# Relative-position bias carried as extra contraction rows of the query and key stacks, with a tanh gate

## The chip, the cores and the metric

One core of one Trainium2 chip runs the kernel. The metric is the device time of the whole launch in microseconds, all 16 batch entries included. Engines are named as the profile names them: PE (TensorE), PEld (its weight loads), DVE (VectorE), ACT (ScalarE), POOL (GpSimd), SP (SyncE, which issues the DMAs).

## The reference

The input x is 16 batches of 16 particles by 48 times by 128 channels. Each batch is one sequence of 768 tokens.

1. LayerNorm over the channels, then attention with 8 heads of 16 dimensions. The score of a query and a key is q·k/4 plus a bias that depends on their time distance plus a bias that depends on their particle distance, each with its own value per head. Keys at a later time than the query are masked. Softmax, product with v, output projection, residual.
2. LayerNorm, then a feed-forward part with 8 experts: softmax over 8 gate logits, the two largest kept and normalised to sum 1. For each of the two weights w, every expert computes GELU(w·x·W1 + b1)·W2, and all are summed. Residual.

## The kernel before

All tokens of a batch lie in time order, so a tile of 128 tokens is 8 times by 16 particles, and there are six tiles. The feed-forward part of one batch is 64 "units" (2 token chunks by 8 experts by 4 slices of the hidden dimension). The attention of the next batch is cut into steps, and a written-out list, `PLAN` (L44 to L66), gives each step the slot (unit number) at which every engine does its share. So the steady state is a loop of 64 slots per batch in which unit work and attention steps alternate in a fixed order on each engine. The first batch's attention runs alone before that loop (it is called the solo batch below), and the last batch's feed-forward part runs alone behind it.

A unit is three matmuls into `zps` (L893 to L895), a multiply on DVE (L727), two GELUs on ACT (L532, L533), an add on POOL (L445) and six matmuls into `acc` (L904).

The attention steps that matter here:

- **stack** (L357): for each of four heads of a group, five DMAs on SP's queue put the head's query and key rows, each as a high and a low fp32r half, in four combinations into `stack` (64 contraction rows, and two rows for the maxima).
- **maxima** (L803 PE, L648 DVE): matmuls give the query-by-key tile without bias. DVE adds the bias and mask from a table `query_table` and takes the row maximum in one custom instruction (L656). Three parts per head, in two PSUM buffers `wide0` and `wide1` that all wide steps use by turns.
- **rows** (L814 PE, L492 ACT, L660 DVE, L377 SP): the maxima of four heads are transposed, negated, split into high and low, and sent by two DMAs into two rows of the query stack.
- **scores** (L817 PE, L496 ACT): key-by-query tiles, three parts per head. Every tile takes two matmuls, one of the stack (L827) and one that adds the bias (L830, one-hot keys times `bias_rows`). ACT takes the exponential (L504). Group 0 stands wholly in slot 26, group 1 in slot 44: no unit work lies between its twelve parts.
- **mix**, **sums**, **divide**, **project**: product with v, denominators, division, output projection.
- **gate**, **weigh**, **split** (L678 to L714): DVE sorts the eight logits and subtracts the largest, ACT takes the exponential (L516), eight small DVE instructions form the two weights, DVE scales xn, PE transposes it (L878, L879) and ACT and DVE split it for the next batch's units.

Ahead of the loop, `query_table` is made by PE and DVE (L764, L576), the bias rows by DVE, POOL and ACT (L560 to L563, L436, L540, L288), and both weights of the experts are loaded.

Of the kernel before, what the change touches and what calls it, by code (L numbers as in the profile page):

```python
# [5 lines left out]
F32 = mybir.dt.float32  # L6
# [3 lines left out]
ALU = mybir.AluOpType  # L10
# [20 lines left out]
STACK_DMAS = 5  # L31
QCOLS = 512
ZW = 2688
NEG = -1e30
LN_EPS = (1e-6, 1e-5)
# [43 lines left out]
VCHAIN = 2 * (5 + 3 * NEWTON) + 7  # L79
# [23 lines left out]
def build(nc, x, Wq, Wk, Wv, Wo, time_bias, part_bias, Wg, W1, b1, W2, b2, out):  # L103
    with ExitStack() as ctx:
# [6 lines left out]
        def sem(name):  # L111
# [15 lines left out]
        bias_rows = sb("bias_rows", [P, GH, TOK], F32R)  # L127
        key_hot = sb("key_hot", [P, GROUPS, P], F32R)
        query_table = sb("query_table", [P, HEADS, TOK], BF16)

# [9 lines left out]
        stack = sb("stack", [P, 2, GH, TOK], F32R)  # L140
        qst, kst = stack[:, 0], stack[:, 1]
# [3 lines left out]
        max_rows = sb("max_rows", [GH * TILES, 2, P])  # L145
# [6 lines left out]
        sorted_l, shifted, gate_e = (halves[:, 3, QCOLS + 48 * n:QCOLS + 48 * (n + 1)].rearrange(  # L152
            "p (i e) -> p i e", e=EXPERTS) for n in range(3))
        gate_s = sb("gate_s", [P, TILES, 4])
        probs = sb("probs", [P, TILES, 2])
# [18 lines left out]
        w1_stage = z[:, 0, 0:2048], z[:, 1, 0:2048]  # L174
        one_hot = z[0:48, 2, 0:128]
        hot_stage = z[0:48, 2, 128:256]

        z_flat = z[:, :, :].rearrange("p g c -> p (g c)")
        raw = [w2[:, 0:GH * TOK // C, :].rearrange("p e d -> p (e d)").rearrange("p (h t) -> p h t", h=GH), z_flat[:, 6912:6912 + GH * TOK].rearrange("p (h t) -> p h t", h=GH)]
        t_stage = z[0:8, 2, 256:256 + 48 * 8]  # L180
        p_stage = z[32:48, 2, 256:256 + 16 * 8]
        b2_stage = z[0:8, 2, 768:896]
        twos = z[0:8, 2, 896:1024]
        b1_stage = z[0:32, 2, 1024:1152]
        rel_stage = z_flat[0:48, 9984:9984 + TOK]
        rel = [rel_stage[:, n * TOK // 2:(n + 1) * TOK // 2].bitcast(BF16) for n in range(2)]

        bias_hi = [w[:, :, :].rearrange("p e f -> p (e f)")[:, 0:GH * TOK].rearrange("p (h t) -> p h t", h=GH)
                   for w in (w1_hi, w1_lo)]
        one_hot16 = z[0:48, 2, 1152:1152 + P // 2].bitcast(BF16)  # L190

        biases_loaded = sem("biases_loaded")
        weights_loaded = sem("weights_loaded")
        w1_high = sem("w1_high")
# [4 lines left out]
        raw_ready = sem("raw_ready")  # L199
        raw_masked = sem("raw_masked")  # L200
        rel_ready = sem("rel_ready")
        bias_high = sem("bias_high")
        bias_low = [sem("bias_low0"), sem("bias_low1")]
        bias_placed = sem("bias_placed")
        table_filled = sem("table_filled")
        table_used = sem("table_used")
        setup_filled = sem("setup_filled")
        setup_done = sem("setup_done")
# [11 lines left out]
        rows_high = sem("rows_high")  # L220
        rows_loaded = sem("rows_loaded")
# [59 lines left out]
        def lower_biases(eng, g):  # L281

            for n, (row, count) in enumerate(((0, TPT), (32, PARTS))):
                eng.wait_ge(bias_high, 2 * g + n + 1)
                if n:
                    eng.wait_ge(bias_low[g], n)
                rows = slice(row, row + count)
                eng.tensor_tensor(raw[g][rows, :, :], raw[g][rows, :, :], bias_hi[g][rows], ALU.subtract).then_inc(bias_low[g], 1)  # L288

# [12 lines left out]
        def _(sp):  # L302
# [13 lines left out]
            for dst, src in ((wqkv[:, 0, :], Wq), (wqkv[:, 1, :], Wk), (wqkv[:, 2, :], Wv), (wg[:, :], Wg)):  # L316
                sp.dma_start(dst, src).then_inc(weights_loaded, 16)
                n += 1
# [81 lines left out]
        def _(pool):  # L400
# [49 lines left out]
            def prepare(r, step, a):  # L450
# [6 lines left out]
                elif (step, a) == ("turn", 1):  # L457
                    for a in range(2):
                        pool.wait_ge(w1_high, a + 1)
                        if a:  # L460
                            pool.wait_ge(w1_low, a)
# [472 lines left out]
```

## Time and profile before

| what | value |
|---|---|
| median of 3 runs | 2730.64 us (2728.61 to 2734.73) |
| the profiled execution's own time | 2739.47 us |
| its span | 2737.6 us |
| mean granted TensorE clock | 0.957 |
| busy share PE, PEld, DVE, ACT, POOL | 87%, 78%, 54%, 62%, 40% |
| the chain that ended last, by engine | PE 57%, DVE 17%, issue 13%, ACT 9%, DMA 2% |

The span runs from the first to the last instruction. A busy share is a mean over stages with different limits, and a pipelined matmul counts as busy from its issue to its modelled end, so that matmuls overlap. "idle before, releaser" in a row is the time that the engine stood still ahead of that instruction, and whose end let it go on. The granted clock is 1.00 at 2.4 GHz and 0.50 at 1.2 GHz.

### The profile page before, as it was taken

The page shows a single profiled execution, that of the slowest core. Times are in us where ns is not written, and L with a number is a line of the kernel's source. Part 1 is how long each engine was busy: PE and PEld are TensorE (multiplying, and loading weights), DVE is VectorE, ACT ScalarE, POOL GpSimd, SP SyncE. Part 2 cuts the span into 40 slices and gives each one's busy share as a digit, 9 for nine tenths or more (in the row PEclk, how much of TensorE's full clock was granted, in tenths as well). Part 3 has the DMA queues.
Part 4 walks back from the last instruction along what each step waited for, and adds up shares of the span by engine and source line. Part 5 has one row for each costly group of instructions (what it writes and reads, how often), then busy time and mean ns, then how long its engine had stood idle before and what let it go on. Part 6 is the DMA issues. An engine that isn't in the chain of part 4 may idle for free.

```text
span 2737.6 us, 57322 instructions
## 1 busy us (share of the span) xinstructions
PE 2377.7 (87%) x18611; PEld 2127.1 (78%) x18611; DVE 1469.6 (54%) x4157; ACT 1695.3 (62%) x2788; POOL 1089.9 (40%) x1054
## 2 busy tenths in 40 slices
PE   1567989899898989989899898989989898998989
PEld 0347878788887878888787878878887787888878
DVE  7536365444735545474554636544573554547454
ACT  2125656675675666666566665667566566756667
POOL 6004244343433434343343424434352443434347
PEclk9678999999999999999999999999999999999999
DMA  2411212040221303022030212203022120302200
GB/s 34 73 38 25 28 28 34 7 52 7 31 28 20 42 7 43 13 34 28 10 49 10 31 25 34 28 8 51 10 28 28 24 38 7 44 12 34 28 10 7
DMA packets 62802, 74.34 MB, mean 27 GB/s; under 512 B 16192, under 2 KB 43744, under 8 KB 62432
## 3 DMA queue, kind: packets, MB, share of 16 engines
q1 hardware_dynamic: 62528, 70.68, 18.4%
q8 instruction: 173, 2.83, 0.4%
q14 instruction: 101, 0.83, 0.1%
HBM read 11.19 MB, written 6.29 MB: 6 GB/s over the span
## 4 chain that ended last, share of the span: by engine, by line
PE 57%; DVE 17%; issue 13%; ACT 9%; DMA 2%; POOL 1%; SPq 1%; DVEq 0%; POOLq 0%; ACTq 0%
PE acc L904 15%; PE wide L827 6%; PE narrow L844 6%; PE zps L893 6%; ACT z L504 5%; PE wide L830 5%; DVE wide L656 5%; PE zps L895 4%; PE zps L894 4%; PE wide L811 4%; DVE h L727 2%; PE wide L865 2%; PE wide L851 1%; DMA stack<-stack 1%; DVE maxes L656 1%
## 5 line engine op out<-in xcount | busy, mean ns | idle before, releaser
L445 POOL TENSOR_TENSOR hsum<-h 128x384 f32<-128x384 f32 x1024 | 1030.2, 1010 | 1491.9 <-ACT h L533 1477.3
L727 DVE TENSOR_TENSOR h<-zps,ratio_b 128x384 f32<-128x384 f32 x1024 | 561.8, 555 | 921.1 <-PE zps L895 917.3
L532 ACT ACTIVATE h<-zps,b_col 128x384 f32<-128x384 f32 x1024 | 594.3, 580 | 662.4 <-DVE h L727 637.1
L904 PE MATMUL acc<-w,hsum 128*128 128x128 f32 x6144 | 867.3, 278 | 1.4 <-DVE outt L736 1.2
L904 PEld LDWEIGHTS acc<-w,hsum 128*128 128x128 f32 x6144 | 850.2, 195 | 2.2 <-POOL hsum L445 1.7
L533 ACT ACTIVATE h<-h,b_col 128x384 f32<-128x384 f32 x1024 | 620.7, 606 | 0.0
L893 PE MATMUL zps<-x_hi,w_lo 128*128 128x384 f32 x1024 | 426.5, 416 | 100.7 <-ACT h L532 57.6
L656 DVE CUSTOM_DVE_ANT_0 wide<-wide,query_table 128x768 f32<-128x768 f32 (+5 forms) x768 | 461.6, 649 | 46.7 <-PE wide L811 44.0
L827 PE MATMUL wide<-stack 128*128 128x256 f32 (+3 forms) x1280 | 374.7, 323 | 69.9 <-ACT z L504 33.9
L504 ACT ACTIVATE z<-wide 128x896 f32<-128x896 f32 (+2 forms) x384 | 345.3, 918 | 95.1 <-PE wide L830 94.3
L894 PE MATMUL zps<-x_lo,w_hi 128*128 128x384 f32 x1024 | 353.4, 345 | 0.0
L895 PE MATMUL zps<-x_hi,w_hi 128*128 128x384 f32 x1024 | 352.6, 344 | 0.0
L830 PE MATMUL wide<-bias_rows,key_hot 128*128 128x256 f32 (+3 forms) x1280 | 351.4, 307 | 0.0
L827 PEld LDWEIGHTS wide<-stack 128*128 128x128 f32 x1280 | 253.1, 198 | 120.0 <-ACT z L504 74.6
L893 PEld LDWEIGHTS zps<-x_hi,w_lo 128*128 128x128 f32 x1024 | 199.2, 195 | 144.1 <-ACT h L532 79.2
L811 PE MATMUL wide<-stack 128*128 128x512 f32 (+3 forms) x1024 | 259.3, 362 | 17.4 <-DVE maxes L656 8.8
L830 PEld LDWEIGHTS wide<-bias_rows,key_hot 128*128 128x128 f32 x1280 | 254.1, 199 | 6.8
L811 PEld LDWEIGHTS wide<-stack 128*128 128x128 f32 x1024 | 168.3, 196 | 43.2 <-DVE maxes L656 20.1
L894 PEld LDWEIGHTS zps<-x_lo,w_hi 128*128 128x128 f32 x1024 | 200.1, 195 | 0.4
L895 PEld LDWEIGHTS zps<-x_hi,w_hi 128*128 128x128 f32 x1024 | 198.1, 193 | 0.0
L844 PE MATMUL narrow<-z,val 128*32 128x256 f32 (+3 forms) x2560 | 175.9, 393 | 3.5 <-ACT mixed L513 1.4
L844 PEld LDWEIGHTS narrow<-z,val 128*32 128x32 f32 x2560 | 82.9, 109 | 87.5 <-issue 21.8
(110 smaller groups left out, 1609.2 us busy)
## 6 DMA issues: line engine op xcount, KB each, us to landing
stack<-halves SPq DMA_DIRECT2D x512, 96.0 KB
x_in<-in_x SPq DMA_DIRECT2D x136, 48.0 KB, 2.4
out_dram<-outt SPq DMA_DIRECT2D x256, 24.0 KB, 1.6
stack<-stack SPq DMA_DIRECT2D x128, 6.0 KB
z<-in_L_ffn_W SPq DMA_DIRECT2D x8, 256.0 KB, 4.2
stack<-max_rows SPq DMA_DIRECT2D x64, 12.0 KB
bias_rows<-w_hi SPq DMA_DIRECT2D x1, 192.0 KB
bias_rows<-w SPq DMA_DIRECT2D x1, 192.0 KB
```

The source lines that it names most:

```text
L445: pool.tensor_tensor(hsum[:, m % NHS, :], h0[:, m % 2, :], h1[:, m % NH1, :], ALU.add).then_inc(hsum_ready, 1)
L532: act.activation(h0[:, m % 2, :], zps[m % 2][:, 0:CT], ACT.Gelu, bias=b1_col[:, j:j + 1]).then_inc(h0_ready, 1)
L533: act.activation(h1[:, m % NH1, :], h1[:, m % NH1, :], ACT.Gelu, bias=b1_col[:, j:j + 1]).then_inc(h1_ready, 1)
L656: ins = vec.tensor_tensor_reduce(w[:, at:at + n], w[:, at:at + n], query_table[:, h, TOK - n:TOK], 1.0, -3e38, ALU.add, ALU.max, maxes[:, ...
L727: vec.tensor_tensor(h1[:, m % NH1, :], zps[m % 2][:, 0:CT], ratio_b[:, c * CT:(c + 1) * CT], ALU.mult).then_inc(z1_ready, 1)
L811: ins = pe.matmul(w[:, at:at + k1 - k0], qst[:, hh, i * P:(i + 1) * P], kst[:, hh, k0:k1], start=True, stop=True)
L827: pe.matmul(w[:, at:at + q1 - q0], kst[:, hh, i * P:(i + 1) * P], qst[:, hh, q0:q1], start=True, stop=False)
L830: ins = pe.matmul(w[:, at:at + q1 - q0], key_hot[:, g, :], bias_rows[:, hh, q0 - i * P:q1 - i * P], start=False, stop=True)
L893: pe.matmul(zp, lo, x0_hi[:, cols], start=True, stop=False)
L894: pe.matmul(zp, hi, x0_lo[:, cols], start=False, stop=False)
L895: pe.matmul(zp, hi, x0_hi[:, cols], start=False, stop=True).then_inc(z_filled, 1)
L904: ins = pe.matmul(acc[:, n * P:(n + 1) * P], hsum[:, k % NHS, n * P:(n + 1) * P], w2[:, j, :], start=(j == 0 and n == 0), stop=(j == UNITS ...
```

## The change

- The query stack becomes eight heads wide (one buffer per head) and holds 127 or 128 contraction rows: 48 rows of data (three high/low combinations in place of four), then bias rows, then one row for the maxima. Time bias: three sets of 16 rows (8 high, 8 low), one for each place of a tile within a half of the tokens. Particle bias: 15 high and 15 low rows. The key stack holds the matching one-hot rows, the same for all batches. A later time has -1e30 in its time row, so the mask is in the product as well.
- The one-hot keys repeat after half of the tokens, so the query stack has a second copy of its second half behind the first, with other time rows; tiles 3 to 5 of the keys meet that copy.
- scores: one matmul per tile. maxima: nine matmuls per head (before eight) with the same number of columns, and a plain maximum on DVE with no table. The six parts of a head are paired so that each part has 896 columns.
- rows: ACT alone, one row, but two DMAs for each head (eight per group). stack: six DMAs for each head. The scores of a head wait only for that head's rows.
- gate: ACT takes tanh of half the difference of the two largest logits; four small DVE instructions in place of eight.
- setup: small tables, spread by ACT and DVE, and placed by 12 DMAs after the solo batch's `value` step; W1 is loaded behind the solo batch's stacks into `w2`, converted on ACT before the solo batch's rows; W2 is loaded after that.

```diff
@@ stack, on SP
-                    for n, (q, k) in enumerate(((0, 2), (1, 2), (0, 3), (1, 3))):
-                        sp.dma_start(stack[n * HD:(n + 1) * HD, :, hh, :].bitcast(F32),
-                                     window(halves[rows, q, :], 0, [[(k - q) * TOK, 2], [1, TOK]])).then_inc(stack_loaded[hh], 16)
-                    sp.dma_start(qst[4 * HD:4 * HD + 2, hh, :].bitcast(F32),
-                                 qst[4 * HD + 2:4 * HD + 4, hh, :].bitcast(F32)).then_inc(stack_loaded[hh], 16)
+                    for n, (q, k) in enumerate(((0, 2), (1, 2), (0, 3))):
+                        to = slice(n * HD, (n + 1) * HD)
+                        sp.dma_start(window(stack[to, :].bitcast(F32), to_q, [[to_k - to_q, 2], [1, TOK]]),
+                                     window(halves[rows, q, :], 0, [[(k - q) * TOK, 2], [1, TOK]])).then_inc(stack_loaded[hh], 16)
+                    for n, q in enumerate((0, 1, 0)):
+                        sp.dma_start(qst[n * HD:(n + 1) * HD, h, TOK:QW].bitcast(F32),
+                                     halves[rows, q, HALF:TOK]).then_inc(stack_loaded[hh], 16)
@@ rows, on SP
-                    for s in range(2):
-                        sp.dma_start(qst[64 + s:65 + s, :, :].bitcast(F32).rearrange("p g (i t) -> p (g i) t", t=P),
-                                     max_rows[:, s, :]).then_inc(rows_loaded, 16)
+                    for hh in range(GH):
+                        row = qst[MAX_ROW:MAX_ROW + 1, a * GH + hh, :].bitcast(F32).rearrange("p (i t) -> p i t", t=P)
+                        sp.dma_start(row[:, 0:TILES, :], max_rows[hh * TILES:(hh + 1) * TILES, :]).then_inc(rows_loaded[hh], 16)
+                        sp.dma_start(row[:, TILES:TILES + HT, :],
+                                     max_rows[hh * TILES + HT:(hh + 1) * TILES, :]).then_inc(rows_loaded[hh], 16)
@@ maxima, on DVE
-                    for i, at in (((5, 0), (1, 768)), ((4, 0), (2, 640)), ((3, 0), (0, 512)))[part]:
-                        n = (i + 1) * P
-                        ins = vec.tensor_tensor_reduce(w[:, at:at + n], w[:, at:at + n],
-                                                       query_table[:, h, TOK - n:TOK], 1.0, -3e38, ALU.add, ALU.max,
-                                                       maxes[:, hh * TILES + i:hh * TILES + i + 1])
+                    for i, at in (((0, 0), (5, P)), ((4, P), (1, 6 * P)), ((3, P), (2, 5 * P)))[part]:
+                        ins = vec.tensor_reduce(maxes[:, hh * TILES + i:hh * TILES + i + 1], w[:, at:at + (i + 1) * P], AX.X, ALU.max)
@@ scores, on PE
-                        pe.matmul(w[:, at:at + q1 - q0], kst[:, hh, i * P:(i + 1) * P], qst[:, hh, q0:q1],
-                                  start=True, stop=False)
-                        ins = pe.matmul(w[:, at:at + q1 - q0], key_hot[:, g, :], bias_rows[:, hh, q0 - i * P:q1 - i * P],
-                                        start=False, stop=True)
+                        shift = HALF if i >= HT else 0
+                        ins = pe.matmul(w[:, at:at + q1 - q0], kst[:, hh, i * P:(i + 1) * P],
+                                        qst[:, g * GH + hh, q0 + shift:q1 + shift], start=True, stop=True)
@@ gate, on ACT
-                    act.activation(gate_e[:, :, :], shifted[:, :, :], ACT.Exp).then_inc(gate_exped, 1)
+                    act.activation(gate_t[:, :], gate_d[:, :], ACT.Tanh, scale=0.5).then_inc(gate_exped, 1)
@@ setup: SP behind the solo batch's value step, DVE behind its LayerNorm
+                if (step, a) == ("value", 0):
+                    sp.wait_ge(times_spread, 1)
+                    ...
+                            sp.dma_start(qst[rows, :, 0:TOK].bitcast(F32), src[:, :, at:at + TOK]).then_inc(bias_placed, 16)
+                            sp.dma_start(qst[rows, :, TOK:QW].bitcast(F32), src[:, :, at:at + HALF]).then_inc(bias_placed, 16)
+                    for h in range(HEADS):
+                        c = h % GH
+                        sp.dma_start(wo_pad[32 * c:32 * c + HD, h // GH, :], Wo[h * HD:(h + 1) * HD, :]).then_inc(wo_loaded, 16)
+                elif (step, a) == ("stack", (0, GH - 1)):
+                    for e in range(EXPERTS):
+                        sp.dma_start(w1_stage[:, e, :], W1[e]).then_inc(w1_loaded, 16)
+                if (step, a) == ("scale", (0, 1)):
+                    vec.tensor_copy(spread[0:40, :, PAD:PAD + TOK].rearrange("p h (t n) -> p h t n", n=PARTS),
+                                    window(t_hl, (TIMES - 1) * HEADS, [[1, HEADS], [-HEADS, TIMES], [0, PARTS]])
+                                    ).then_inc(times_spread, 1)
```

## Rows read from the trace of the kernel before

**Rows 1.** The page's part 5, groups: busy us, mean ns, idle before, releaser

```profile
L656 DVE CUSTOM_DVE_ANT_0 wide<-wide,query_table 128x768 f32<-128x768 f32 (+5 forms) x768 | 461.6, 649 | 46.7 <-PE wide L811 44.0
...
L504 ACT ACTIVATE z<-wide 128x896 f32<-128x896 f32 (+2 forms) x384 | 345.3, 918 | 95.1 <-PE wide L830 94.3
...
L830 PE MATMUL wide<-bias_rows,key_hot 128*128 128x256 f32 (+3 forms) x1280 | 351.4, 307 | 0.0
```

**Rows 2.** The chain that ended last: project step, second and last, 14 apart

```profile
351.82 2.68 PE wide L865 x24
...
2620.81 2.68 PE wide L865 x24
```

**Rows 3.** Timeline of ACT in one round's scores of group 1: start, us

```profile
1296.66 1.68 ACT L504 ACTIVATE z<-wide 128x896 f32<-128x896 f32 x2
...
1302.14 1.92 ACT L504 ACTIVATE z<-wide 128x1024 f32<-128x1024 f32 x2 [0.19 <-PE wide L830]
1304.39 0.81 ACT L504 ACTIVATE z<-wide 128x768 f32<-128x768 f32 x1 [0.34 <-PE wide L830]
...
1308.65 1.02 ACT L504 ACTIVATE z<-wide 128x1024 f32<-128x1024 f32 x1 [0.19 <-PE wide L830]
```

**Rows 4.** Timeline of PE in the same round's scores of group 0

```profile
1252.72 0.33 PE L827 MATMUL wide<-stack 128*128 128x256 f32 x1
...
1253.61 0.28 PE L830 MATMUL wide<-bias_rows,key_hot 128*128 128x256 f32 x1
1253.79 0.50 PE L827 MATMUL wide<-stack 128*128 128x512 f32 x1
...
1254.54 0.34 PE L830 MATMUL wide<-bias_rows,key_hot 128*128 128x384 f32 x1
```

**Rows 5.** Windows: length, busy and count by engine, granted clock, DMA share, GB/s

```profile
1246.00:1248.00 2.00, 2.00 (x9) 1.68 (x8) 0.00 (x0) 1.02 (x1) 0.00 (x0) 0.50 0.00 0
...
1302.00:1304.00 2.00, 1.88 (x12) 1.46 (x11) 0.00 (x0) 1.86 (x2) 0.00 (x0) 1.00 0.00 0
...
148.00:152.00 4.00, 2.96 (x9) 2.15 (x8) 3.43 (x12) 0.00 (x0) 0.00 (x0) 0.50 0.00 0
```

**Rows 6.** Timeline of DVE in the same round's maxima of group 1

```profile
1286.17 0.95 DVE L656 CUSTOM_DVE_ANT_0 wide<-wide,query_table 128x768 f32<-128x768 f32 x1
...
1287.04 0.46 DVE L656 CUSTOM_DVE_ANT_0 wide<-wide,query_table 128x256 f32<-128x256 f32 x1
```

**Rows 7.** Timeline around the gate of the same round

```profile
1180.84 1.28 ACT L532 ACT_TABLE_LOAD   x1 [0.32 <-DVE h L727]
...
1182.77 0.45 PE L893 MATMUL zps<-x_hi,w_lo 128*128 128x384 f32 x1 [0.97 <-ACT h L532]
...
1184.07 0.27 PE L878 MATMUL wide<-ident,xn 128*128 128x128 f32 x1
```

**Rows 8.** Timeline of SP's queue and PE at the first stack of a round

```profile
1207.33 2.58 SPq L372 DMA_DIRECT2D stack<-halves  x4
...
1214.26 0.74 PE L811 MATMUL wide<-stack 128*128 128x512 f32 x3 [0.29 <-DMA stack<-stack]
```

**Rows 9.** Timeline of the setup and the solo batch

```profile
7.12 4.22 DVE L560 COPY w<-z 8x3072 f32<-8x3072 f32 x1 [7.12 <-POOL z L423]
...
36.95 1.26 DVE L611 BATCH_NORM_STATS2 act_t<-x_in 128x6 f32<-128x128 f32 x6
...
86.82 2.16 PE L811 MATMUL wide<-stack 128*128 128x512 f32 x6 [5.87 <-issue]
...
106.66 0.27 ACT L494 ACTIVATE max_rows<-wide 24x128 fp32r<-24x128 f32 x1 [42.34 <-PE wide L816]
...
201.08 3.00 DVE L686 TENSOR_TENSOR halves<-halves 128x48 f32<-128x48 f32 x1
...
204.85 3.83 DVE L692 TENSOR_TENSOR probs<-halves,gate_s 128x12 f32<-128x12 f32 x1
```

**Rows 10.** The page's part 6, DMA issues: KB each, us to landing

```profile
z<-in_L_ffn_W SPq DMA_DIRECT2D x8, 256.0 KB, 4.2
```

More of the change, by code:

```diff
@@ L30 @@
 NHS = 4
-STACK_DMAS = 5
 QCOLS = 512
@@ L34 @@
 NEG = -1e30
+STACK_DMAS = 6
+HALF = TOK // 2
+QW = TOK + HALF
+TIME_ROWS = (48, 79, 111)
+PART_ROWS = (64, 96)
+PART_N = PARTS - 1
+MAX_ROW = 127
+PAD = 2 * P
 LN_EPS = (1e-6, 1e-5)
@@ L151, in build @@
         ln_t = sb("ln_t", [P, TILES])
[L152 to L155, printed above, removed]
+        sorted_l = halves[:, 3, QCOLS:QCOLS + 48].rearrange("p (i e) -> p i e", e=EXPERTS)
+        gate_d = sb("gate_d", [P, TILES])
+        gate_t = sb("gate_t", [P, TILES])
+        gate_r = sb("gate_r", [P, TILES])
         top = sb("top", [P, TILES, 2])
@@ L279, in rounds @@
             slots(Round(eng, BATCHES - 1), None, None)
[L281 to L288, printed above, removed]
         def wide_at(r, step, a):
@@ L426, in _ @@
             assert done == POOL_SMALL
+            pool.wait_ge(biases_loaded, 16 * BIAS_LOADS)
+            for row in (0, 32):
+                v = t_tab[row:row + TPT, :].rearrange("p (m h) -> p m h", h=HEADS)
+                pool.affine_select(out=v, in_=v, compare_op=ALU.is_ge, fill=NEG, base=TIMES - 1,
+                                   pattern=[[-1, TIMES], [0, HEADS]], channel_multiplier=-1).then_inc(tables_masked, 1)
             for buf, value in later:
@@ new lines, in _ @@
+            for row in (0, 32):
+                rows = slice(row, row + PART_N)
+                vec.tensor_tensor(p_diff[rows, :], p_tab[rows, :], p_first[rows, :], ALU.subtract).then_inc(parts_less, 1)
+            vec.wait_ge(tables_high, 2)
+            vec.tensor_tensor(t_hl[32:32 + TPT, :].bitcast(F32R), t_tab[32:32 + TPT, :], t_hl[32:32 + TPT, :],
+                              ALU.subtract).then_inc(tables_low, 1)
+            vec.wait_ge(tables_high, 4)
+            vec.tensor_tensor(p_hl[32:32 + PART_N, :].bitcast(F32R), p_diff[32:32 + PART_N, :], p_hl[32:32 + PART_N, :],
+                              ALU.subtract).then_inc(tables_low, 1)
@@ L741, in after @@
                         residual(r, 1)
-            rounds(vec, attention, unit, after, last=("stats", "seed", "root", "scale", "rows"), prepare=prepare)
+            rounds(vec, attention, unit, after, last=("stats", "seed", "root", "scale"), prepare=prepare)
         @block.tensor
@@ L755, in prepare @@
             def prepare(r, step, a):
[L756 to L769 removed]
+                if (step, a) == ("value", 0):
+                    pe.wait_ge(pool_set, POOL_SET)
+                    pe.wait_ge(hots_placed, 16 * HOT_DMAS)
+                    pe.wait_ge(parts_spread, GROUPS)
+                    pe.wait_ge(bias_placed, 16 * BIAS_DMAS)
+                elif (step, a) == ("divide", 1):
+                    pe.wait_ge(wo_loaded, 16 * HEADS)
                 elif (step, a) == PLAN[-1][1:]:
```

269 lines of the change are left out of this document (105 added, 164 removed).

## The prediction

> **What bounds the kernel now.** I read the groups of part 5 first, then the chain that ended last over the whole run and in one steady round, and then the timelines of the stages that the change touches. The groups name three things to follow [rows 1]. ACT's exponential stood idle for 94 us waiting for the bias matmul L830. L830 itself is 351 us of busy PE. The custom maximum on DVE is 462 us. The chain gives the round: 2269.0 us between the first and the last project step of the loop, 14 rounds, so 162.07 us each [rows 2]. Fifteen rounds carry an attention; the solo batch ahead of them and the last feed-forward part behind them make up the rest.
>
> A round is a chain of stages with different limits. In the stages with unit work alone, PE and ACT are both full. In scores nothing lies between the parts: ACT and PE hand two buffers to each other, and the four heads of group 1 take 1308.65 + 1.02 - 1296.66 = 13.01 us, 3.25 per head [rows 3]. In that stage ACT waits 0.34 us ahead of the 768-wide part and 0.19 ahead of the 1024-wide one, so it is the sum of both engines that sets the pace: a buffer is filled, read, and only then filled again. Over two heads each buffer is used three times. Its 6.5 us are three exponentials (the 2.75 us that three times the mean of 918 ns give), three fills, and the hand-overs.
>
> **The change, part by part.**
>
> *Scores, one matmul per tile.* The 1024-wide part has eight matmuls and takes 1253.61 + 0.28 - 1252.72 = 1.17 us, with 0.127 us from one start to the next (0.89 over seven); the 896-wide part has four and takes 1254.54 + 0.34 - 1253.79 = 1.09 us [rows 4]. Half of the matmuls and half of the columns go. In the 1024-wide part that is 4 x 0.127 = 0.51 us; 896 columns at 2.4 GHz are 0.37 us, the lower bound. I take 0.42 per fill. Three fills in two heads: 0.63 us per head, from 3.25 to 2.62. ACT's own floor is near it: 1.68 for two parts back to back plus 1.02 for the third is 2.70, less about 0.05 for each overlap of one with the next (0.92 + 0.81 against 1.68), so 2.6 [rows 3]. Four heads: 2.5 us for each group. Group 1 also waits for its first fill with nothing before it: another 0.4. Group 0 has its first 0.9 us or more of exponential behind a table load, so none there. Together 5.4 us per round; bounds 4.4 (fills cut by 0.37) and 6.3 (by 0.51, ACT nearly never waiting).
>
> This part depends on the clock. In group 0 PE already drops to 0.50 for some microseconds in the middle of scores, after standing idle behind the table load, and comes back with PE busy all the time; in group 1 it stays at 1.00 with 1.88 of 2.00 us busy; and in the solo batch's maxima it stays at 0.50 with 2.96 of 4.00 us busy [rows 5]. With half of the matmuls gone PE has 2688 columns, 1.12 us, to stream in 2.6 us. That is less work than any stretch of a round that I found at 1.00, and this is the second rival below.
>
> *Maxima.* The same 2688 columns per head in nine matmuls in place of eight: on PE one more start, a few hundredths of a us per head, nothing in the sum. On DVE the bias table goes, not the elements: 768 elements advance it by 1287.04 - 1286.17 = 0.87 us [rows 6], 0.80 of it at one element per 0.96 GHz cycle. A plain reduction reads the same elements. No row shows one of that size; the plain multiply L727 with the same kind of operands takes 0.47 us start to start for 384, so the overhead is about the same, 0.07. Below: 0.05 us saved for each of 24 instructions of a group, 1.2 us; above: nothing saved. In group 1 DVE is full from the first part to the last, with L727 between, so I take 0.6 us there. In group 0 PE is full as well: nothing. The read-accumulator records overlap the next instruction and are no gain.
>
> *Rows.* The DVE step (0.3 us) leaves a chain that group 1 waits for: 0.3 us per round. The first head's two DMAs are as many as before. The other six come on SP's queue behind them at about 0.65 us each (2.58 for four [rows 8]), 1.3 us per head against 2.6 of exponentials: hidden. If each DMA landed 1.3 us late it would show as ACT waiting at the second head.
>
> *Stack.* Six DMAs in place of five, 3.9 us of SP per head in place of 3.3, and 360 KB in place of 390. Group 0's first maxima already come 0.29 us behind that landing, 6.9 us after the first issue [rows 8]. The bytes set it more than the issues, so I count nothing; bounds -0.3 and +0.6 us per round. In group 1 SP now falls behind scores (3.9 against 2.6 per head) and ends some 5 us after them; the maxima of head 1 are then still in slot 33. Queued behind are only the next rows and loads.
>
> *Gate.* ACT loads the table of the exponential before it and that of GELU after it. The first load lies in ACT's wait for DVE. The second does not: it starts at 1180.84, takes 1.28, the GELU behind it releases PE's unit at 1182.77, and PE's split, queued behind that unit, starts at 1184.07 [rows 7]; ACT and DVE then split it for the next chunk, with PE idle until they end. If tanh needs no load of its own, the unit comes 1.28 us earlier. DVE's four short instructions fewer, 0.2 us each, take 0.8 off the other way into split, which ends about half a us ahead of the unit, so both fall by about 1.2. If tanh needs a load, the unit is as late as before and the gain is 0.1. No row shows tanh. Copies run between GELUs without a load and the exponential does not, so a function can be on either side; I take 1.2, at something above even odds. On this a page speaks against: the Trainium skill, "ScalarE: Activation LUTs", the section "Table sets: the hidden batching unit", lists tanh with the exponential's and sigmoid's sets and names only gelu in gelu's. By that rule both loads stay and the time would be that of the first rival. The trace agrees only as far as exponential and GELU are in different sets.
>
> *A round:* 5.4 + 0.6 + 0.3 + 1.2 = 7.5 us, times 15 is 112 us.
>
> *Setup.* Before, the solo batch's LayerNorm starts at 36.95 behind 30 us of table copies on DVE, and its maxima at 86.82, behind the query table [rows 9]. After, DVE has four tiny instructions first. I let LayerNorm start at about 10 (x and tables landed), xn ready at 16, as 6 us pass now. Then DVE spreads 6144 elements at the price of L560 (4.22 us for 3072 [rows 9]): 8.4, to 25; the key halves follow at about 26. SP can then issue 12 bias DMAs, 8 for Wo, and 6 for the first head: 26 x 0.65 = 17 us, to 43, with 1.8 MB of bias rows moving meanwhile (16 us at the 110 GB/s of the stack DMAs). First maxima at about 46, 41 us earlier. They take 20 us, DVE bound: to 66. ACT, however, stands before the rows waiting for W1: SP issues W1 behind the stacks, at about 56, 2 MB (eight of 256 KB, each 4.2 us to landing [rows 10]) need some 10 to 12, and two casts 4. So rows come at about 71 rather than 106.66 [rows 9]: 35 us. Behind it: scores 5 us (eight heads), and at the gate 7: L686 and L692 took 3.00 and 3.83 us while POOL lowered W1, against 0.2 each in other rounds [rows 9], and that POOL work now lies in the solo scores. Together 47 us. If the bias DMAs move half as fast, 30; if W1 is not waited for, 55.
>
> *Sum:* 112 + 47 = 159 us off the profiled execution's 2739.5: 2580. The median of the runs is 8.8 below that execution: 2572.
>
> **Rivals.**
>
> 1. *The table loads stay.* Everything else as above, 15 x 1.1 = 16 us back: 2588. For it: nothing in the profile says that tanh goes with GELU. Chance 0.20.
>
> 2. *PE's clock falls in scores.* At 1.2 GHz the halved fill costs nearly what the full one costs now at 2.4, so scores stay near 3.2 per head, and the mix behind them starts slow (2.5 us for 48 matmuls now). If half of the stretch is spent low I get 1.5 us per round in place of 5.4: 15 x 3.9 = 58 back, 2630. For it: [rows 5], above all that group 0 enters with the clock about to fall. Against: with few columns PE still has a matmul or a weight load in flight for most of the time, and no wait is over 0.6 us. Chance 0.21. The Trainium skill says the same in "TensorE: Matmul & The Clock Gate", section "A second HAM failure mode: psum-queue depth-cycling": groups of matmuls that cycle through PSUM buffers with short idle times between can make the clock swing between its two levels. In the rounds traced here it did not in group 1.
>
> 3. *DVE's plain maximum is dearer: slower.* Place: both maxima stages. At twice the custom instruction's price a head costs 6.7 us in place of 3.4. Group 0, where a head has 4.9 us of PE beside 1.4 of L727 on DVE, loses 4 x 3.2 = 13, group 1 another 13.5; less 8 that the rest gives (the maxima's own gain falls away) this is about 19 us per round, and the time 2990. It decides from about 1.4 times the price. Against it: one element per cycle is what every DVE instruction on PSUM here shows. Chance 0.03.
>
> 4. *The removed matmuls were not what ACT waited for*, because each exponential is released through semaphores and not by the fill: scores keep 3.25. Then 15 x 5.4 + 5 come back: 2658. Against it: the two gaps of ACT differ with the part. Chance 0.03.
>
> **How the numbers follow.** The forecast has 0.53. Its own range is 2540 to 2606: 17 us for a setup gain of 30 to 55 or so, and 15 us each way for the scores' bounds and the maxima's, which I don't expect at one end together. The range for all cases is 2535 to 2640: it holds the first two rivals and leaves out the last two, some of the second, and a little of the forecast's own edge, below 2 in 10. About 0.2% (5 us) is what a measurement can tell from no change. Slower holds rival 3 and as much again for a new wait that I have not seen; all else is faster by over 2%: faster 0.94, same 0.01, slower 0.05.
>
> **What the profile of the changed kernel would show.** In scores of group 1: ACT's four heads in 10.5 us, gaps of at most 0.1 us, and the granted clock at 1.00 (rival 2: 0.50 in windows of scores and of the mix behind them; rival 4: gaps as now). ACT_TABLE_LOAD: none at the tanh and one less per round at L532's successor (rival 1: as many as now). The reduction of 768 elements: 0.9 to 0.97 us (rival 3: 1.3 or more). Project to project: 154.5 us. First maxima near 46, first rows near 71 with ACT's wait ended by W1. The prediction is wrong in a way that I have not listed if PE waits for stack or rows DMAs in every round, or if setup takes as long as before because the 12 bias DMAs, with eight source partitions each, crawl.

## The result and the profile after

The changed kernel takes 2685.95 us (median of 4 runs, 2684.27 to 2693.18) against 2730.82 (2728.61 to 2734.73) for the kernel before: 0.984 of its time, 95% interval 0.982 to 0.986. It is 45 us faster where 159 were forecast, and lies outside the range. The gain is clear of noise but only 1.6%: the prediction had counted a gain under 2% as "same" and given it 0.01, and had given 0.94 to more than 2%.

The head of its page: the span, the busy time by engine, and the groups that the change touches (columns as in [rows 1]).

```profile
span 2691.2 us, 54396 instructions
...
PE 2328.3 (87%) x17443; PEld 2071.1 (77%) x17443; DVE 1373.4 (51%) x3267; ACT 1661.6 (62%) x2760; POOL 1050.5 (39%) x1048
...
L633 DVE TENSOR_REDUCE maxes<-wide 128x1 f32<-128x128 f32 (+5 forms) x768 | 437.3, 616 | 87.5 <-PE wide L769 83.8
L784 PE MATMUL wide<-stack 128*128 128x256 f32 (+3 forms) x1280 | 348.9, 432 | 108.2 <-ACT z L490 82.9
...
L490 ACT ACTIVATE z<-wide 128x896 f32<-128x896 f32 (+2 forms) x384 | 343.5, 916 | 63.8 <-PE wide L784 54.9
```

Against [rows 1]: the bias matmul is gone, but the exponential still waits 55 us for PE (94 before), and the matmul that is left (L784) takes 432 ns in the mean, where its like in the kernel before (L827) took 323 and the removed one (L830) 307:

```profile
L827 PE MATMUL wide<-stack 128*128 128x256 f32 (+3 forms) x1280 | 374.7, 323 | 69.9 <-ACT z L504 33.9 <-DMA stack<-max_rows 27.9
```

The mean granted clock fell from 0.957 to 0.897. So PE does less, at a lower clock, and its busy share is the same 87%. In a round the clock stands at 0.50 for 27.3 us (mean of 14); in the kernel before it was 7.8.

From one project step of the loop to the next it is now 160.44 us in the mean of 14 (160.3 to 160.7), against 162.07 (160.7 to 163.2) [rows 2]. The first project step of the loop starts at 327.91 instead of 351.82. So the span's 46.4 us are 14 x 1.63 = 22.8 and, ahead of the first such step, 23.9; the last part is 0.2 longer.

ACT's timeline in one round's scores of group 1 answers to [rows 3]:

```profile
1424.34 3.58 ACT L490 ACTIVATE z<-wide 128x896 f32<-128x896 f32 x4
1428.32 0.81 ACT L490 ACTIVATE z<-wide 128x768 f32<-128x768 f32 x1 [0.40 <-PE wide L784]
...
1432.56 1.88 ACT L490 ACTIVATE z<-wide 128x1024 f32<-128x1024 f32 x2 [0.24 <-PE wide L784]
1434.79 0.81 ACT L490 ACTIVATE z<-wide 128x768 f32<-128x768 f32 x1 [0.34 <-PE wide L784]
1435.75 1.02 ACT L490 ACTIVATE z<-wide 128x1024 f32<-128x1024 f32 x1 [0.16 <-PE wide L784]
```

Four heads take 1435.75 + 1.02 - 1424.34 = 12.43 us (13.01 before, 10.5 forecast). The first four exponentials run without a gap, as forecast for all twelve. Then the gaps of before are back. The windows of the same stretch, and below them those of group 0, say why (columns as in [rows 5]):

```profile
1424.00:1426.00 2.00, 0.69 (x4) 0.53 (x4) 0.00 (x0) 1.95 (x3) 0.10 (x1) 1.00 0.02 4
1426.00:1428.00 2.00, 1.52 (x7) 1.13 (x7) 0.00 (x0) 1.83 (x2) 0.00 (x0) 0.77 0.00 1
...
1430.00:1432.00 2.00, 1.94 (x8) 1.63 (x8) 0.00 (x0) 1.71 (x3) 0.00 (x0) 0.50 0.00 0
...
1434.00:1436.00 2.00, 2.00 (x11) 1.62 (x13) 0.00 (x0) 1.50 (x3) 0.00 (x0) 0.50 0.00 0
1436.00:1438.00 2.00, 2.00 (x18) 0.60 (x16) 0.00 (x0) 0.78 (x1) 0.00 (x0) 0.67 0.00 0
...
1372.00:1374.00 2.00, 0.00 (x0) 0.00 (x0) 0.00 (x0) 1.97 (x3) 1.14 (x2) 1.00 0.02 4
...
1378.00:1380.00 2.00, 1.94 (x6) 1.09 (x6) 0.00 (x0) 1.82 (x3) 0.00 (x0) 0.50 0.88 95
```

PE is busy for 0.69 and 1.52 of 2.00 us and the granted clock goes from 1.00 to 0.50, in both groups, and stays there into the mix. PE's 1.94 at 0.50 are eight matmuls in 2 us, where the kernel before did twelve in 1.88 at 1.00 [rows 5]: PE looks as busy, with less work done. In each of the 14 rounds the clock is at 0.50 for 10.2 us in group 0 and for 10.2 in group 1. In the kernel before, group 1 stayed at 1.00 in all of them, and group 0 fell for 3.4 us in eight. In the chain the first piece of the mix behind it is

```profile
1435.72 3.67 PE narrow L798 x30
```

and in the kernel before these matmuls, at full clock, stood in the chain with 2.3 us.

**Setup.** SP's queue, then what PE and ACT waited for (answers to [rows 9]):

```profile
28.41 2.96 SPq L324 DMA_DIRECT2D stack<-z  x1
31.42 1.97 SPq L325 DMA_DIRECT2D stack<-z  x1
33.43 3.78 SPq L324 DMA_DIRECT2D stack<-z  x1
...
54.78 2.00 SPq L325 DMA_DIRECT2D stack<-z  x1
56.83 8.51 SPq L328 DMA_DIRECT2D wo_pad<-in_L_conv_Wo  x8
65.39 1.94 SPq L359 DMA_DIRECT2D stack<-halves  x3
...
70.97 1.51 PE L769 MATMUL wide<-stack 127*128 127x128 f32 x4 [36.82 <-DMA stack<-halves]
...
90.90 3.70 ACT L526 CAST w_hi<-w 128x2048 fp32r<-128x2048 f32 x2 [55.92 <-DMA w<-in_L_ffn_W]
94.51 0.26 ACT L480 ACTIVATE max_rows<-wide 24x128 fp32r<-24x128 f32 x1
```

The bias DMAs hold SP's queue for 30 us: twelve were issued from 26.92 to 56.78, and most stand in it for 3.8 us (192 KB) or 2.0 us (96 KB), not for 0.65. The window 40 to 60 us shows that no engine worked meanwhile (from 56.83 on Wo's DMAs are in it as well):

```profile
40.00:60.00 20.00, 0.00 (x0) 0.00 (x0) 0.00 (x0) 0.00 (x0) 0.00 (x0) 0.50 0.46 50
```

The DMA engines are busy for 0.46 of the time and move 50 GB/s. So the first maxima come at 70.97, not at 46.

### The profile page after: what moved, and what is told of

Same layout as the page of the kernel before. It is cut to its first block, busy times and chain, and to the rows that moved or that the text cites. A ratio compares the mean times of both kernels' runs of the same rounds, so it can differ in the third digit from the quotient of the medians.

```text
span 2691.2 us, 54396 instructions
## 1 busy us (share of the span) xinstructions
PE 2328.3 (87%) x17443; PEld 2071.1 (77%) x17443; DVE 1373.4 (51%) x3267; ACT 1661.6 (62%) x2760; POOL 1050.5 (39%) x1048
## 4 chain that ended last, share of the span: by engine, by line
PE 64%; issue 12%; DVE 11%; ACT 9%; SPq 2%; POOL 1%; DMA 0%; DVEq 0%; ACTq 0%; POOLq 0%
PE acc L858 18%; PE wide L784 9%; PE narrow L798 7%; PE zps L847 7%; PE zps L848 5%; PE zps L849 5%; ACT z L490 5%; PE wide L769 5%; DVE maxes L633 3%; DVE h L691 2%; PE wide L812 2%; PE wide L819 2%; PE wide L805 1%; ACT L490 1%; ACT h L519 1%
## 5 line engine op out<-in xcount | busy, mean ns | idle before, releaser
L518 ACT ACTIVATE h<-zps,b_col 128x384 f32<-128x384 f32 x1024 | 593.5, 580 | 678.4 <-DVE h L691 659.2
L633 DVE TENSOR_REDUCE maxes<-wide 128x1 f32<-128x128 f32 (+5 forms) x768 | 437.3, 616 | 87.5 <-PE wide L769 83.8
L784 PE MATMUL wide<-stack 128*128 128x256 f32 (+3 forms) x1280 | 348.9, 432 | 108.2 <-ACT z L490 82.9
L784 PEld LDWEIGHTS wide<-stack 128*128 128x128 f32 x1280 | 264.1, 284 | 187.4 <-ACT z L490 159.0
L769 PE MATMUL wide<-stack 127*128 127x384 f32 (+2 forms) x1152 | 266.5, 346 | 41.6 <-DMA stack<-halves 37.8
L769 PEld LDWEIGHTS wide<-stack 127*128 127x128 f32 x1152 | 182.1, 196 | 55.9 <-issue 40.2
L848 PEld LDWEIGHTS zps<-x_lo,w_hi 128*128 128x128 f32 x1024 | 206.0, 201 | 0.4
L798 PE MATMUL narrow<-z,val 128*32 128x256 f32 (+3 forms) x2560 | 185.2, 417 | 1.3 <-ACT mixed L499 1.3
L747 PE MATMUL wide<-ident,xn 128*128 128x128 f32 x192 | 34.2, 326 | 74.3 <-DVE xn L618 39.3
L747 PEld LDWEIGHTS wide<-ident,xn 128*128 128x128 f32 x192 | 24.6, 160 | 79.9 <-issue 67.8
```

Source lines behind the costliest of these rows:

```text
L518: act.activation(h0[:, m % 2, :], zps[m % 2][:, 0:CT], ACT.Gelu, bias=b1_col[:, j:j + 1]).then_inc(h0_ready, 1)
L633: ins = vec.tensor_reduce(maxes[:, hh * TILES + i:hh * TILES + i + 1], w[:, at:at + (i + 1) * P], AX.X, ALU.max)
L769: ins = pe.matmul(w[:, at:at + k1 - k0], qst[0:MAX_ROW, h, q0:q0 + P], kst[0:MAX_ROW, hh, k0:k1], start=True, stop=True)
L784: ins = pe.matmul(w[:, at:at + q1 - q0], kst[:, hh, i * P:(i + 1) * P], qst[:, g * GH + hh, q0 + shift:q1 + shift], start=True, stop=True)
L848: pe.matmul(zp, hi, x0_lo[:, cols], start=False, stop=False)
```

## The experiments

Ten kernels ran, each the changed kernel with an edit. A matmul whose result nobody reads is called idle below. Times of a "project step" here are those of its DVE record, about 2.7 us behind PE's start.

**keep: an idle matmul behind each scores part.**

```diff
@@ scores, on PE, rounds of the loop only
+                    if steady and hh == 0 and part == 0:
+                        pe.wait_ge(narrow_free, r.at(NPB, NARROW["mix", (g, 0)]))
 ...
+                    if steady:
+                        pe.matmul(narrow[:, 0:512], w1_hi[:, 0, 0:P], w1_hi[:, 0, 0:512], start=True, stop=True)
```

> The changed kernel with one extra 512-column matmul behind each scores part, into the PSUM buffer of mix, whose result nobody reads; it leaves nothing out. Theory A (the granted clock took the gain): PE has enough to do in scores, the clock stays at 1.00 for group 1 at least, four heads of group 1 take about 10.6 us in place of 13.1, and mix 2.3 us in place of 3.7. Group 0, which enters with the clock about to fall, gains less. 2 to 4.5 us per round, 2620 to 2655 us. Theory B (ACT's pace in scores is set by something other than PE's fill, such as the semaphores or the stack DMAs): heads keep 3.27 us or grow by the 0.2 us of each extra matmul, 2686 us or more, whatever the clock.

Measured: 2617.55 us (2616.48 to 2618.9), 0.9585 of the time before (0.9562 to 0.9607); rounds of 155.76; granted clock 0.954. That is theory A: more work on PE makes the kernel 68 us faster. At 0.50 a round now spends 7.6 us. ACT's timeline in scores of group 1 of one round, and two windows of it:

```profile
1386.72 10.77 ACT L490 ACTIVATE z<-wide 128x896 f32<-128x896 f32 x12
```

```profile
1386.00:1388.00 2.00, 0.66 (x4) 0.35 (x4) 0.00 (x0) 1.99 (x3) 0.49 (x1) 1.00 0.01 2
1390.00:1392.00 2.00, 2.00 (x12) 1.34 (x10) 0.00 (x0) 1.93 (x3) 0.00 (x0) 1.00 0.00 0
```

All twelve exponentials stand in one piece of 10.77 us without a gap: the prediction's 10.5 for group 1, reached once the clock is 1.00. Group 1 is so in 13 of 14 rounds. Group 0 is in five; in the other nine it takes 11.7 to 11.9 us, the clock falls to 0.50 for 3.4 us, and there are one or two gaps of 0.4 to 0.6 us near its start, as the expectation had it. The first window has PE busy for only 0.66 of 2.00 us, no more than in the changed kernel, and the clock stays up; the next 2 us have 1.75 with twelve matmuls, where the changed kernel had 1.52 with seven.

**cover: keep, and eight more idle matmuls behind the first head of each group**, to help the mix as well.

> As the first, with eight more of these matmuls behind the second scores part of a group, where PE stands still 2.5 us while ACT loads the exponential's table. Theory A: the clock does not fall at the head of group 0 either, both groups take 10.6 us, 4 to 5.5 us per round, 2600 to 2625 us. If the idle time behind the table load is not what brings the clock down, no gain over the first. Theory B: as for the first, 2686 us or more.

Measured: 2621.96 (2620.18 to 2622.52), 0.9601 (0.9578 to 0.9624). From the first exponential to the first mix copy, group 0 took 13.48 us in the mean of 14 rounds (14.12 in keep) and its clock never fell; group 1 took 13.51 (13.32). So the idle time behind the table load was what lowered the clock in group 0. But the stretch from `x_lo` to the rows of group 0, which the edit does not touch, took 49.16 (48.45), and the round 156.02. Why it is longer is open; one idle matmul is enough.

**twice: each scores matmul issued twice.** The product is the same, and PE's work is that of before, without the bias table.

```diff
-                        ins = pe.matmul(w[:, at:at + q1 - q0], ...)
+                        for _ in range(2):
+                            ins = pe.matmul(w[:, at:at + q1 - q0], ...)
```

> The changed kernel with each scores matmul issued twice into the same place (the second overwrites the first), which puts PE's work in scores back to what it was before the change. Theory A: the clock is 1.00 in group 1, heads take 3.25 us as before the change, mix 2.3 us; so within a few us per thousand of the changed kernel: about 1 to 1.5 us per round slower, 2690 to 2710 us. Theory B: the same price as the changed kernel, 2686. If one pass had given its full 5.4 us per round, 2765 us.

Measured: 2691.14 (2690.2 to 2692.94), 0.9854 (0.9831 to 0.9877), clock 0.956, rounds of 160.41 against 160.44. From exponential to mix it takes 16.27 and 15.51 us in the mean, as in the kernel before (16.07, 15.51). So halving PE's work in scores bought 5 us by the medians and nothing in a round: 0.98 us that the changed kernel gains from exponential to mix, it loses again between `x_lo` and the rows of group 0 (49.79 against 48.78), with the clock at 0.50 for longer there (6.8 us from project to rows against 5.6). The 1.63 us that a round did gain is there with every scores matmul issued twice.

**keep_small: as keep, with 256 columns.**

> As the kernel with one idle 512-column matmul behind each scores part, with 256 columns. Theory A: if half of the extra work is enough, the clock in scores is 1.00 as there and the time the same within 5 us of 2618 us; if not, windows of 0.50 come back in scores and the time lies between 2618 and 2686 us. Theory B (the extra matmul helps in another way than by the clock) says nothing on the size.

Measured: 2618.05 (2613.08 to 2623.59), 0.9593 (0.9575 to 0.9611), rounds of 155.55. The time does not differ from keep's. So half as many idle columns are enough for it, though the clock is a little lower (0.948 against 0.954).

**expgate: the exponential in place of tanh**, of minus the difference. The weights are 1/(1+e) and e/(1+e); DVE has as many instructions.

```diff
-                    act.activation(gate_t[:, :], gate_d[:, :], ACT.Tanh, scale=0.5)...
+                    act.activation(gate_t[:, :], gate_d[:, :], ACT.Exp, scale=-1.0)...
```

> The changed kernel with the gate's tanh undone: ACT takes exp of minus the difference, DVE the same number of short instructions. Two more table loads per round. Theory A (the load was hidden: split waits for DVE's x_lo, which is queued behind the next batch's statistics): 0 to 0.4 us per round, 2686 to 2692 us. Theory B (the forecast's: the load of GELU's table lies on the path): 1.2 us per round, 2704 us.

Measured: 2671.39 (2666.72 to 2673.91), 0.9777 (0.9751 to 0.9804): faster by 14.6 us, which neither theory had. The loads are there. By form, the first line of the two kernels' table loads at the gate and the GELU, of the changed kernel first:

```profile
L518 ACT ACT_TABLE_LOAD x31 | 39.8, 1283 | 26.6 <-DVE h L691 26.6
```

```profile
L518 ACT ACT_TABLE_LOAD x46 | 59.0, 1283 | 32.3 <-DVE h L691 32.3
...
L502 ACT ACT_TABLE_LOAD x15 | 19.2, 1283 | 0.3
```

Two more loads in each round of expgate, and the split's `x_lo` comes at 23.46 us after the project step where the changed kernel has 23.92. So the saved loads were off the path. Of the profiled span's 19.1 us, 6.6 lie in the solo batch (its project step at 165.64, not 172.24), whose instructions up to there are the same, and 10.4 in the fourteen later rounds (159.70 against 160.44): three of them are near 157.5 and the others at 160.1 to 160.5. This looked like the clock and not like the function. best2_exp below tests it.

**order: LayerNorm of the next batch one slot later**, so that it doesn't stand ahead of `x_lo` on DVE.

```diff
-    plan = [(-5, "stats", 0), (-5, "seed", 0), (-4, "root", (0, 0)), (-4, "root", (0, 1)), (-4, "root", (0, 2)),
-            (-3, "scale", (0, 0)), (-2, "scale", (0, 1)),
+    plan = [(-4, "stats", 0), (-4, "seed", 0), (-3, "root", (0, 0)), (-3, "root", (0, 1)), (-3, "root", (0, 2)),
+            (-2, "scale", (0, 0)), (-2, "scale", (0, 1)),
```

> The changed kernel with the next batch's statistics one slot later, behind split, so that DVE's x_lo is not queued behind them. Theory A (what hid the tanh gate's gain is DVE's queue at split): PE's next unit after split comes up to 2 us earlier after project (23.9 us to x_lo now, 21.5 to 22.5 then), and the round 0.5 to 2 us shorter if the LayerNorm, which now starts later, does not hold up turn; 2656 to 2680 us. Theory B (LayerNorm is then late for turn and gives it back): 2683 to 2692 us.

Measured: 2689.78 (2687.67 to 2690.66), 0.985 (0.9833 to 0.9866). `x_lo` comes 0.7 us earlier (23.25), the query step no earlier (40.6 to 40.9, before the edit 40.3 to 40.6), the rounds stay at 160.41 and the last part, without a next batch, is 3.2 us longer. Theory B.

**sixteen: bias DMAs of 16 partitions.** A DMA of 12 KB moves the low rows beside the high ones, and six DMAs of 16 partitions take the place of twelve of eight; the bytes are the same.

```diff
-                        for half in range(2):
-                            rows, src = slice(to + half * TPT, to + (half + 1) * TPT), spread[32 * half:32 * half + TPT]
+                        rows, src = slice(to, to + 2 * TPT), spread[0:2 * TPT]
@@ ACT, before the spread
+            act.dma_start(t_hl[TPT:2 * TPT, :], t_hl[32:32 + TPT, :]).then_inc(lows_moved, 16)
```

> The changed kernel with the low time rows moved by a 12 KB DMA beside the high ones in the staging table, so that six bias DMAs with 16 source partitions take the place of twelve with 8. Theory A (a DMA from 8 partitions moves at half the rate, 50 GB/s as the windows from 28 to 58 us show, and SP stands in the queue behind it): bias rows done by about 45 us in place of 60, first maxima at 56 in place of 71, and the whole 13 to 16 us faster, 2670 to 2673 us. Theory B (the 3 KB pieces or the issues set the rate, whatever the partitions): no change beyond 3 us.

Measured: 2669.51 (2667.52 to 2672.4), 0.9778 (0.9762 to 0.9794): 16.4 us less than the changed kernel. SP's queue and the first maxima, and the DMA engines in a window of it:

```profile
34.29 3.76 SPq L324 DMA_DIRECT2D stack<-z  x1
38.09 2.03 SPq L325 DMA_DIRECT2D stack<-z  x1
40.16 8.59 SPq L328 DMA_DIRECT2D wo_pad<-in_L_conv_Wo  x8
48.80 1.88 SPq L359 DMA_DIRECT2D stack<-halves  x3
...
54.42 1.94 PE L771 MATMUL wide<-stack 127*128 127x128 f32 x6 [19.45 <-DMA stack<-halves]
```

```profile
30.00:40.00 10.00, 4.97 (x19) 2.95 (x17) 1.91 (x2) 2.42 (x3) 0.00 (x0) 0.98 0.90 99
```

One DMA stands in SP's queue as long as before but carries twice the bytes: share 0.90 and 99 GB/s, where it was 0.46 and 50. The Trainium skill, "DMA: Bandwidth & Descriptors", section "Why a DMA increments its semaphore by 16 and not by 1", says that as many engines share a DMA, up to 16, as divide both sides' outermost size; by it eight partitions reach half of the engines. The trace agrees, 0.46 against 0.90.

**best: all of it** (keep, cover in group 0 alone, order, sixteen, and W1's conversion on ACT behind the solo batch's first mix).

```diff
@@ the conversion, W1 on ACT and on POOL
-                if (step, a) == ("value", 0):
+                if (step, a) == ("mix", (0, 1)):
```

> All together: idle 512-column matmuls behind each scores part and eight more at the table load of group 0 alone, the 16-partition bias DMAs, statistics behind split, and the solo batch's W1 conversion moved from ahead of its rows to behind its first mix. Sum by the parts: 68 us from the first (2618), 15 from the bias DMAs, 6 from the conversion (rows no longer wait for W1 from 88.6 to 94.5 us), 0 to 20 from the order: 2577 to 2600 us.

Measured: 2613.94 (2613.02 to 2618.8), 0.9576 (0.9558 to 0.9593): only 4 us below keep, and above the 2577 to 2600 that were expected. The parts ahead of the loop gained what they should (rows at 72.44; second project step at 297.44, 24.6 less than keep where 21 were expected), but a round takes 156.94 and the last part 117.65 us where the changed kernel's has 114.32. The clock stays at 1.00 in scores and mix of both groups, which take 13.48 and 13.26 us in every round; but from `x_lo` to the rows of group 0 it takes 51.13, 2.7 more than in keep.

**best2 and best2_exp: without order and cover.** keep_small, sixteen and the moved conversion; the second with expgate's edit as well.

> The changed kernel with the three edits that paid by themselves and none that did not: one idle matmul of 256 columns behind each scores part (keep_small: 2618.05), 16-partition bias DMAs (sixteen: 16.4 us less), and W1's conversion moved behind the solo batch's first mix (rows of the solo batch came at 72.4 in the run best, against 77.1 in sixteen). The plan is that of the changed kernel. Theory A (the three lie in different stretches and add): 2618 - 16 - 4 = 2598, 2590 to 2605, rounds of 155.6, second project near 298. Theory B (what the combined run best lost was not the plan of the gate but an interplay of setup and rounds): 2614 or more, with rounds of 156.5 or more.

> best2 with the exponential of minus the difference in place of tanh (as many DVE instructions, the division left as in expgate, two more table loads per round). Theory A (the 14.6 us by which expgate was faster than the changed kernel came from a luckier phase of the clock in its scores and solo batch, not from the function): with the clock kept up, within 5 us of best2. Theory B (the exponential itself is the better choice, since the small DVE instructions behind it meet less of POOL): 8 to 15 us faster than best2, and rounds shorter by 0.6 to 0.8 us. Theory C (the table loads cost 1.1 us a round, as the prediction had it): 16 us slower.

Measured: best2 2597.9 us (2597.04 to 2600.39), 0.9511 (0.9493 to 0.9529), rounds of 155.98, second project step at 300.3. best2_exp 2600.74 (2599.16 to 2608.59), 0.9528 (0.9503 to 0.9553), rounds of 156.02. So the three edits add, and what best lost was order, or order with cover. With the clock kept up tanh and the exponential are the same within what can be measured: in best2_exp `x_lo` comes at 23.45 and not at 23.91, and the round is no shorter. best2 is the fastest kernel of this study, 133 us faster than the one before and 88 faster than the changed one.

## Why the prediction was wrong

Times in us between stages, from the DVE record of one project step to the next, means of the 14 rounds of each trace:

| stretch | before | after | difference | forecast | keep | twice |
|---|---|---|---|---|---|---|
| project to x_lo (gate) | 24.19 | 23.92 | -0.27 | -1.2 | 23.93 | 23.92 |
| x_lo to rows of group 0 | 49.56 | 49.79 | +0.23 | 0 | 48.45 | 48.78 |
| rows to first exponential, groups 0 and 1 | 6.28, 4.99 | 6.25, 4.86 | -0.16 | -0.7 | 6.25, 4.86 | 6.25, 4.86 |
| exponential to first mix copy, group 0 | 16.07 | 15.59 | -0.48 | -2.5 | 14.12 | 16.27 |
| the same, group 1 | 15.51 | 15.21 | -0.30 | -2.5 | 13.32 | 15.51 |
| mix of group 0 to rows of group 1 (maxima) | 30.99 | 30.36 | -0.63 | -0.6 | 30.36 | 30.36 |
| mix of group 1 to project | 14.48 | 14.47 | -0.01 | 0 | 14.46 | 14.46 |
| round | 162.07 | 160.44 | -1.63 | -7.5 | 155.76 | 160.41 |

The forecast of 0.4 for group 1's first fill stands with the rows' 0.3, since that fill lies ahead of the first exponential.

1. **Scores, the step that failed.** "Three fills in two heads: 0.63 us per head" was worked out at a clock of 1.00. The mechanism was right: in best, where the clock stayed at 1.00 in both groups, they took 13.48 and 13.26 us, 2.6 and 2.25 less than before, 4.8 together where 5.0 were forecast (in keep, with some falls left, 4.1). The size was not, because the removed matmuls were also what had held the clock: in the changed kernel 0.78 came. The text knew it ("less work than any stretch of a round that I found at 1.00") and gave it 0.21. Its argument against, that a matmul or a weight load is in flight for most of the time, does not hold: in the windows above PE was busy for 0.69 and 1.52 of 2.00 us ahead of the fall, and PEld for 0.53 and 1.13. [rows 5] already had such a window, the solo maxima at 0.50 with PE busy for 2.96 of 4.00, and so 1.48 of 2.00; it should have made rival 2 the likeliest. Rival 2 left 1.5 us per round of the scores' gain; half of that was measured. Against keep the clock cost 4.68 us a round (160.44 against 155.76), 65.5 us over 14 rounds: 1.5 and 1.9 in the two groups, and 1.3 between `x_lo` and the rows of group 0, where keep has no edit. The Trainium skill's "TensorE: Matmul & The Clock Gate", section "A second HAM failure mode: psum-queue depth-cycling", which was named for rival 2, is what the trace shows here: two levels, with short idle times between two PSUM buffers.

2. **Gate.** That tanh needs no load was right: L518 has 31 loads, L502 none, 46 and 15 in expgate. Here the table of "ScalarE: Activation LUTs" in the Trainium skill, section "Table sets: the hidden batching unit", was contradicted. The step "so both fall by about 1.2" was wrong; 0.27 came, and expgate, with the loads back, has `x_lo` earlier, not later. What is late next is DVE's and ACT's order. In the gate of one round of the changed kernel (lines of PE, DVE and ACT):

```profile
1313.42 0.33 PE L832 MATMUL wide<-ident,xn 128*128 128x128 f32 x1 [0.37 <-DVE xn L665]
...
1314.22 1.24 DVE L589 BATCH_NORM_STATS2 act_t<-x_in 128x6 f32<-128x128 f32 x6
...
1315.88 0.47 ACT L509 CAST x_hi<-wide 128x384 fp32r<-128x384 f32 x1
...
1316.51 0.57 DVE L597 TENSOR_SCALAR ln_v<-moments 128x6 f32<-128x6 f32 x1
...
1317.43 0.56 DVE L670 TENSOR_TENSOR x_lo<-wide,x_hi 128x384 fp32r<-128x384 f32 x1
```

PE's transposes start earlier, ACT's `x_hi` then stands behind the GELUs of two units, and DVE's `x_lo` behind the next batch's LayerNorm. PE's wait ahead of the next unit is 3.16 us. order took the LayerNorm away: `x_lo` came 0.7 earlier and the round was no shorter. Nor was it in best2_exp, with `x_lo` 0.46 earlier than in best2. A gain here is used up behind it: in order before the query step, in best2_exp before the rows of group 0 (48.85 us from `x_lo`, 48.44 in best2).

3. **Maxima and rows.** Maxima as forecast. The reduction of 768 elements took 946 ns (968 for the custom instruction), so rival 3 is out. Rows and group 1's first fill gave 0.16 instead of 0.7. PE's waits for DMAs did not grow: 18.6 us of the scores matmuls' waiting is put down to the rows (27.9 before), and of the 37.8 us of waiting for stacks 36.8 is the one in setup.

4. **Setup and solo batch.** Forecast 47 and one round's 7.5, 54.5 together; measured 23.9. The 30.6 that lack: 22.8 at the solo rows (94.51, 12.2 earlier instead of 35), 1.4 in its scores (3.6 instead of 5), and 6.4 in the first round (8.1 instead of 7 + 7.5), which is the steady term again; the gate's 7 came (25.50 to 17.94 us from project to `x_lo`). The failed step is "26 x 0.65 = 17 us, to 43": the bias DMAs needed 30 and Wo's eight 8.5, so the first maxima came 25 us later than forecast. From there to the rows it took 23.54 where 25 were forecast, the wait for W1 included. The last line of the prediction's text had named it (the DMAs "crawl"), but the bound for it, a gain of 30 in all, was too kind: Wo's and the stacks' issues come behind the bias rows and not beside them. sixteen returned 16.4 us. And the spread on ACT had no term in the sum at all:

```profile
9.52 17.33 ACT L537 CAST stack<-z 47x4608 fp32r<-47x4608 f32 x2 [0.35 <-DVE z L560]
26.88 0.80 ACT L469 COPY act_t<-wide 128x768 f32<-128x768 f32 x1
```

The spread of the particle rows holds ACT for 17.3 us and the solo batch's `act_t` waits behind it. SP waits for it too: DVE's spread was done at 22.11 (3.35 us, 8.4 in the forecast), but SP stood for another 5 us until ACT's was, and issued the first bias DMA at 26.92. That this is the forecast's 26 is luck, two errors that cancel. Moving the spread was not tried.

**The balance.** Forecast 159, measured 46.4 in span. Rounds: 14 x (7.5 - 1.63) = 82.2. Setup and first round: 30.6. Together 112.8, against 112.6 that lack. Of the 82.2, keep returned 65.5. The prediction had a price for each of the three errors (58 for the clock, 16 for the gate, 17 for slow DMAs, 91 together), but its range took them one at a time.

Rival 4 (the removed matmuls were not what ACT waited for) is out by keep: with the clock up, the gaps are gone.

## What to carry to other kernels

Work taken from PE in a stage where PE alternates with another engine can come back as a lower clock: before counting on the gain, look in the old trace for stretches as thin as the coming one, and forecast at the clock that they had. Where it falls, an idle matmul into a free PSUM buffer in each gap can be worth more than the edit that opened the gap (here 68 us against 45). No run put idle matmuls into the kernel before, whose group 0 also fell in eight of 14 rounds, so how much of keep's 2617.55 needs the change at all is not known. A saved instruction counts only if what follows it in its engine's queue is awaited: follow it to the next step that PE waits for.

## What the runs showed of the hardware

**The phase of the clock is worth microseconds in identical code.** The solo batch's instructions are the same in the changed kernel and in order, yet its second scores and mix ran at different clocks (windows of the changed kernel, then of order, which is 2 us ahead by then, so that they do not hold quite the same instructions):

```profile
142.00:166.00 24.00, 21.41 (x171) 14.77 (x174) 0.31 (x1) 11.07 (x14) 0.00 (x0) 0.64 0.31 89
```

```profile
142.00:166.00 24.00, 19.66 (x193) 13.86 (x192) 1.54 (x3) 9.51 (x12) 0.00 (x0) 0.86 0.31 88
```

The solo project step came at 172.24 and at 165.72. It can differ within one kernel as well: the changed kernel's profiled execution is its slowest, 2693.18 us at a clock of 0.897, and the other three took 2684.27 to 2687.05 at 0.901 and 0.902; and in keep's 14 rounds the same instructions from `x_lo` to the rows of group 0 took 47.5 to 50.0 us. A small edit elsewhere can so show 5 to 7 us that are not its own. It is the likely cause of expgate's gain, which is not shown, though best2_exp speaks for it; what decides the phase is open.

**ACT's spread of the particle rows is dear:** 47 x 4608 elements took 8.7 us each, 1.9 ns per element of a partition, where the exponential on 1024 takes 1.02 us, 1.0 ns. It reads a small table again and again and writes fp32r; which of its traits costs the time no run separates. DVE's spread of 6144 took 3.35 us, against 4.22 for 3072 in [rows 9], so the price of L560 was not its price either.

**An SBUF to SBUF DMA of eight partitions moves at half speed, and the queue behind it waits for that:** 192 KB from eight partitions hold SP for 3.8 us at 50 GB/s, and in sixteen 384 KB from 16 partitions hold it for 3.76 at 99 GB/s. SP stands only from the third bias DMA on: the first two took it 0.7 us each. Wo's eight small ones, behind the last, hold it for 8.5 together.
